# Q and K made in two halves of heads, the second half between the first head's maximum chunks

## What is computed

```
x = x + graph0(norm(x))            # adj @ (norm(x) * W)
h = norm(norm(x)) * g + b
q, k, v = h @ wq + bq, h @ wk + bk, h @ wv + bv     # 8 heads of 32 columns
attn = softmax(q @ k.T / sqrt(32)) # for each head, 1354 x 1354
x = x + ... + (attn @ v) @ wo + bo, then a mixture of 8 experts
x = x + graph1(norm(x)), x = x + experts(norm(x))
```

## Time and profile before

| what | value |
|---|---|
| three runs | 1010.37 us median (1009.64 to 1010.59) |
| the profiled execution's own time | 1012.66 us |
| its span in the trace | 1010.9 us |
| PE, DVE, ACT, POOL busy | 828.1, 518.7, 385.4, 104.5 us |
| granted TensorE clock, mean | 0.899 |

### The profile page before, as it was taken

One profiled execution on the slowest core, in us unless ns is written; L12 is line 12 of the kernel. 1 busy time (PEld: TensorE's weight loads), 2 busy tenths in 40 slices (PEclk: granted clock), 3 DMA queues, 4 the chain that ended last, 5 costly groups with the idle time before them and its releaser, 6 DMA issues.

```text
span 1010.9 us, 12855 instructions
## 1 busy us (share of the span) xinstructions
PE 828.1 (82%) x3873; PEld 578.3 (57%) x3874; DVE 518.7 (51%) x1075; ACT 385.4 (38%) x788; POOL 104.5 (10%) x92
## 2 busy tenths in 40 slices
PE   4968799999999996229999456974449999999993
PEld 4855555555555435129999354862316666666663
DVE  4035587666666748628889237966412222222220
ACT  1004415556555564006666234312013444444441
POOL 2000000000000000160000310000621111111111
PEclk9998859999999999659999777997569999999996
DMA  7498720233321110042442473407231222222212
GB/s 260 148 274 306 209 51 19 69 79 72 77 71 27 36 29 9 10 150 94 166 177 103 144 300 128 143 21 312 78 109 28 32 33 34 32 32 32 32 26 65
DMA packets 53654, 101.57 MB, mean 100 GB/s; under 512 B 17614, under 2 KB 46054, under 8 KB 51920
## 3 DMA queue, kind: packets, MB, share of 16 engines
q1 hardware_dynamic: 47328, 92.20, 28.6%
q0 software_dynamic: 6288, 8.89, 4.9%
HBM read 70.80 MB, written 25.35 MB: 95 GB/s over the span
## 4 chain that ended last, share of the span: by engine, by line
PE 72%; issue 10%; DVE 8%; DMA 4%; ACT 2%; POOL 1%; SPq 0%; POOLq 0%; ACTq 0%; DVEq 0%
PE ps L1167 11%; PE ps L929 11%; PE ps L1149 10%; PE ps L909 6%; PE ps L860 5%; PE ps L921 5%; PE ps L1098 4%; PE ps L1014 4%; PE ps L1016 3%; PE ps L1015 3%; PE ps L1158 3%; DVE mx L1306 2%; PE ps L1113 1%; PE ps L848 1%; PE ps L1075 1%
## 5 line engine op out<-in xcount | busy, mean ns | idle before, releaser
L1306 DVE TENSOR_REDUCE mx<-ps 128x1 f32<-128x452 f32 x264 | 148.1, 621 | 67.3 <-PE ps L909 66.0
L715 ACT ACTIVATE expo<-ps 128x452 f32<-128x452 f32 x264 | 124.3, 551 | 110.4 <-PE ps L921 109.5
L929 PE MATMUL ps<-expo,v_st 128*64 128x452 f32 (+1 forms) x576 | 116.4, 526 | 0.0
L1167 PE MATMUL ps<-w_l,h 128*128 x464 | 110.4, 392 | 7.2 <-ACT h L831 4.1
L909 PE MATMUL ps<-k_st,q_st 96*128 96x452 f32 x264 | 111.3, 451 | 3.5 <-DMA k_st<-k_hi_d 3.3
L831 ACT ACT_TABLE_LOAD x29 | 37.2, 1283 | 190.6 <-PE ps L1158 190.6
L1149 PE MATMUL ps<-w_l,x1t_t 128*128 x232 | 106.0, 600 | 1.7 <-DVE x1t_t L1600 1.7
L1167 PEld LDWEIGHTS ps<-w_l,h 128*128 128x128 f32 x464 | 87.7, 194 | 25.8 <-issue 14.6
L921 PE MATMUL ps<-q_st,k_st 98*128 98x452 f32 x264 | 96.7, 387 | 2.0 <-ACT expo L715 2.0
L1612 DVE COPY h1pre<-ps 128x1024 f32<-128x1024 f32 x29 | 35.5, 1225 | 107.4 <-PE ps L1149 107.4
L909 PEld LDWEIGHTS ps<-k_st,q_st 96*128 96x128 f32 x264 | 54.4, 207 | 50.5 <-DVE mx L1306 35.1
(11 more groups left out here) (230 smaller groups left out, 1233.2 us busy)
## 6 DMA issues: line engine op xcount, KB each, us to landing
w_l<-w_l SPq DMA_DIRECT2D x8, 2053.0 KB, 8.4
w_l<-w_l SPq DMA_DIRECT2D x2, 8208.0 KB, 23.6
adj<-adj_t SPq DMA_DIRECT2D x22, 704.0 KB, 4.2
xs_d<-zeros SPq DMA_DIRECT2D x1, 3842.5 KB, 26.3
x1t<-xs_d SPq DMA_DIRECT2D x29, 132.5 KB, 2.1
q_st<-q_hi_d SPq DMA_DIRECT2D x16, 176.0 KB, 3.2
k_st<-k_hi_d SPq DMA_DIRECT2D x16, 176.0 KB, 4.2
xs_d<-zeros SPq DMA_DIRECT2D x1, 2176.0 KB, 10.5
```

The costliest lines, as they stand in the source:

```text
L715: act.activation(expo[g % 8][:, :], ps[:, 3 + g % 3, 0:QC], ACT.Exp, scale=SCALE).then_inc(s_exp, 1)
L929: return pe.matmul(ps[at:at + 2 * DK, 6 + g // T % 2, lo:hi], v_st[h % 2][:, kt, :], expo[g % 8][:, lo:hi], start=kt < 2, stop=kt == T - 1 ...
L1167: mm = pe.matmul(ps[:, 6, 0:D], h1[:, f, :], w_l1[:, bass.ds(e, 1), at:at + D].rearrange("p a n -> p (a n)"), start=f == 0, stop=f == FT - 1)
L1306: dve.tensor_reduce(mx4[:, n // KB, n % KB:n % KB + 1], ps[:, i % 3, 0:KC], AX_X, ALU.max).then_inc(s_mx, 1)
```

## The change

Q's and K's chunks are ordered by block of heads: eight chunks of heads 0 to 3 (HALF), then eight of heads 4 to 7. All tiles of a chunk have three buffers.

- First half: ACT writes `proj_hi` from PSUM at once, and DVE makes `proj_lo` from PSUM with one scalar_tensor_tensor (bias added, high part subtracted). `proj` isn't written. ACT waits for the stores of the chunk three places earlier.
- SP waits for the first half's stores alone and loads stacks 0 and 1. V's products follow the first half's on PE.
- Second half: PE makes a product, then four maximum slots of head 0 (BESIDE), and so on eight times; then the ten slots that are left. ACT writes `proj` and `proj_hi`, two instructions a chunk, and GpSimd subtracts. These stores stand on SP behind `load_values`, and stack 2 behind them and behind `load_max(0)`.
- ACT loads the table of exponentials ahead of the second half (a 128x1 Exp), waits for all stores ahead of the first exponentials, and PE waits for all high parts ahead of the first scores.

```diff
+        qk_chunks = [(hi_d, lo_d, mt, c) for mt in range(DT) for hi_d, lo_d in ((q_hi_d, q_lo_d), (k_hi_d, k_lo_d))
+                     for c in range(QB)]
+        HALF = len(qk_chunks) // 2
+        def qk_bank(n):
+            return n if n < HALF else 3 + (n - HALF) % 5
+        BESIDE = 4
...
+            for n in range(HALF):
+                store_qk(n)
+            stored(HALF)
...
             load_values(1, 1)
+            for n in range(HALF, 2 * HALF):
+                store_qk(n)
+            load_max(0)
             load_stack(2)
-            load_max(0)
...
-            pool.wait_ge(s_v_ps, T)
+            for n in range(HALF, 2 * HALF):
+                pool.wait_ge(s_qk_hi, n + 1)
+                pool.tensor_tensor(proj_lo[n % 3][:, :], proj[n % 3][:, :], proj_hi[n % 3].bitcast(F32)[:, :],
+                                   ALU.subtract).then_inc(s_qk_lo, 1)
...
+            def qk_high(n):
                 act.wait_ge(s_qk_ps, n + 1)
+                if n >= 3:
+                    act.wait_ge(s_qk_out[n % 3], 32 * (n // 3))
+                for lo, hi, bank in qk_pieces(n):
+                    if n >= HALF:
+                        act.activation(proj[n % 3][:, lo:hi], ps[:, bank, 0:hi - lo], ACT.Identity, bias=qk_bias(n))
+                    last = act.activation(proj_hi[n % 3][:, lo:hi], ps[:, bank, 0:hi - lo], ACT.Identity, bias=qk_bias(n))
+                last.then_inc(s_qk_hi, 1)
...
+            act.activation(psum_e[:, 0:1], ones[:, 0:1], ACT.Exp).then_inc(s_table, 1)
+            for n in range(HALF, 2 * HALF):
+                qk_high(n)
+            act.wait_ge(s_table, 1)
+            for k in range(3):
+                act.wait_ge(s_qk_out[k], 32 * len(range(k, 2 * HALF, 3)))
...
-            for i in range(FILL):
+            for n in range(HALF, 2 * HALF):
+                qk_product(n)
+                for i in range((n - HALF) * BESIDE, (n - HALF + 1) * BESIDE):
+                    fill_slot(i)
+            for i in range(HALF * BESIDE, FILL):
                 fill_slot(i)
+            pe.wait_ge(s_qk_hi, 2 * HALF)
...
+            def qk_low(n):
                 dve.wait_ge(s_qk_hi, n + 1)
+                for lo, hi, bank in qk_pieces(n):
+                    last = dve.scalar_tensor_tensor(out=proj_lo[n % 3][:, lo:hi], in0=ps[:, bank, 0:hi - lo], scalar=qk_bias(n),
+                                                    in1=proj_hi[n % 3].bitcast(F32)[:, lo:hi], op0=ALU.add, op1=ALU.subtract)
+                last.then_inc(s_qk_lo, 1)
```

More of the change, by code:

```diff
@@ L185, in build_program @@
         cursor[0] = offsets["expo0"]
-        proj = [place(f"proj{i}", [NC4]) for i in range(2)]
-        proj_hi = [place(f"proj_hi{i}", [NC4], F32R) for i in range(2)]
-        proj_lo = [place(f"proj_lo{i}", [NC4], F32R) for i in range(2)]
+        proj = [place(f"proj{i}", [NC4]) for i in range(3)]
+        proj_hi = [place(f"proj_hi{i}", [NC4], F32R) for i in range(3)]
+        proj_lo = [place(f"proj_lo{i}", [NC4], F32R) for i in range(3)]
         assert cursor[0] <= offsets["ctx_raw0"]
@@ L290, in build_program @@
         s_qk_ps = sem("qk_product_done")
-        s_qk_raw = sem("qk_biased")
         s_qk_hi = sem("qk_high_ready")
+        s_table = sem("exp_table_wanted")
         s_qk_lo = sem("qk_low_ready")
-        s_qk_out = [sem(f"qk_written{i}") for i in range(2)]
+        s_qk_out = [sem(f"qk_written{i}") for i in range(3)]
         s_v_ps = sem("v_product_done")
@@ L392, in build_program, with qk_pieces, qk_bias @@
         s_b2_add = sem("b2_added")
-        qk_chunks = [(hi_d, lo_d, mt, c) for hi_d, lo_d in ((q_hi_d, q_lo_d), (k_hi_d, k_lo_d))
-                     for mt in range(DT) for c in range(QB)]
+        qk_chunks = [(hi_d, lo_d, mt, c) for mt in range(DT) for hi_d, lo_d in ((q_hi_d, q_lo_d), (k_hi_d, k_lo_d))
[3 more added lines that the diff above has]
+            return n if n < HALF else 3 + (n - HALF) % 5
+        def qk_pieces(n):
+            hi_d, lo_d, mt, c = qk_chunks[n]
+            if hi_d is q_hi_d or c < QB - 1:
+                return ((0, NC4, qk_bank(n)),)
+            return ((0, N - c * NC4, qk_bank(n)), (N - c * NC4, NC4, qk_bank(n - c)))
+        def qk_bias(n):
+            hi_d, lo_d, mt, c = qk_chunks[n]
+            v = (V_BQ if hi_d is q_hi_d else V_BK) + mt
+            return vecs[:, v:v + 1]
         w_l0_b2 = [b[:, FT:FT + DT] for b in b_l0]
@@ L693, in _ @@
             turned(0, V_G1, V_B1)
-            for n, (hi_d, lo_d, mt, c) in enumerate(qk_chunks):
-                v = V_BQ if hi_d is q_hi_d else V_BK
+            def qk_high(n):
                 act.wait_ge(s_qk_ps, n + 1)
[L699 to L704, removed]
-                if pads:
-                    last = act.activation(proj[n % 2][:, real:NC4], ps[:, (n - c) % 8, 0:NC4 - real], ACT.Identity,
-                                          bias=vecs[:, v + mt:v + mt + 1])
-                last.then_inc(s_qk_raw, 1)
+                if n >= 3:
[5 more added lines that the diff above has]
+                last.then_inc(s_qk_hi, 1)
+            for n in range(HALF):
+                qk_high(n)
             def exps(g):
```

38 lines of the change are left out of this document (21 added, 17 removed).

## The result

The changed kernel takes 995.63 us (median of 4 runs, 994.92 to 998.45), the kernel before 1010.0 on the same chip (1007.89 to 1010.59). The ratio is 0.9865, with a 95% interval of 0.9846 to 0.9884: 14.4 us or 1.35% faster. The forecast was 994.5, in 991.5 to 999.5. So its gain by the medians is 14.4 us in the one measurement and 11.4 in the other. The profiled execution took 995.35 us for a span of 993.6, against a span of 1010.9 before. Two executions further on, one of direct16 (1477.88 us) and one of stack2 (2149.08), count in the medians but not in the ratios, and why they were slow is open.

A forecast was written before the change was run, and what follows sets the result against it. Two stretches ahead of the attention, not set by the matmul rate, bound the kernel: stores, then row maxima. Scores 13.4 us earlier plus 2.5 by the clock made 15.9, giving 994.5 us from the median, range 991.5 to 999.5.

The forecast's parts named there:

- first rival: The forecast itself, clock full throughout: 994.5 us, own range 993 to 996; chance 0.50.
- The first stack's issue: First half of Q and K: last store lands at 99.4, so the first stack is issued 15.9 us earlier.
- Issue to first slot: Path from the first stack's issue to PE's first slot: kept at 6.83 us, first slot at 106.2.
- PE's waits: Before the first slot, V and one product keep PE busy until 106.0, so it waits for about nothing.
- Rival 4: PE waits over 3 us for the stack and falls to half clock: 1000.2 to 1008.2 us; chance 0.08.
- Slots with products between: Head 0's slots: seven products between them lose 0.4 us each, 2.8 in all; bounds nothing to 14.
- GpSimd, chunk 15, the table, stack 2: Off the path: subtraction 0.9 us, chunk 15 lands at 128.8 with 3 us cover, table loaded early, stack 2 needed later.
- rival 7: Second half's stores land late and hold up the first exponential, making the kernel slower; chance 0.03.
- The clock at the first scores: First score to second group of value products: at full clock 7.2 us instead of 9.75, gaining 2.5.
- the row of 388 to 391: Sign for a full clock through the last 14 slots: PE busy 1.12 of 3 us there, yet at 1.00.
- rival 2: Clock falls in the last 14 slots, scores begin at half clock: 2.5 us less gain, 997.0; chance 0.24.
- The sum: Whole kernel: 13.4 us from earlier first scores plus 2.5 from the clock, 15.9 us faster.

The follow-up runs named there:

- direct16: Kernel before plus only the three buffers and direct casts, all 16 chunks in the old order: 1004.72 us against 1009.53, ratio 0.9947.
- stack2: Changed kernel with stack 2 loaded ahead of head 0's maxima, as before the change: 998.49 us, ratio 0.9896 to the kernel before.
- again: Changed kernel measured once more, unchanged: 997.28 us against 1008.66 for the kernel before, ratio 0.9892.
- first: Changed kernel with all second-half products ahead of the slots, not between them: 1002.13 us, ratio 0.9928 to the kernel before.
- dvelow: Changed kernel with the second half's low parts made by DVE from PSUM between the maxima: 997.22 us, ratio 0.9886 to the kernel before.
- b3warm: Changed kernel with three slots between products and an added product behind each of the last 18 slots: 990.96 us, ratio 0.9824 to the kernel before.
- notable: Changed kernel without the early Exp that loads the exponential table: 998.02 us, ratio 0.9903 to the kernel before.
- beside5: Changed kernel with five slots between products instead of four: 996.56 us, ratio 0.9881 to the kernel before.
- w0late: b3warm with the first two 2 MB loads of second-layer expert weights moved behind the stacks: 990.11 us, ratio 0.9816 to the kernel before.
- buf2: Changed kernel with two buffers instead of three for the high, low and biased tiles: 1000.53 us, ratio 0.9919 to the kernel before.
- beside3: Changed kernel with three slots between products instead of four: 992.6 us, ratio 0.9851 to the kernel before.
- warm: Changed kernel with one added, unread product behind each of the last ten slots: 993.01 us, ratio 0.9846 to the kernel before.

## Why the prediction was right, and where not

The time was forecast at 994.5 and came at 995.6 and 997.3, in the range and on the side that was said. Two of its steps were off, and the measured times lie between its first rival and its second.

**The first stack's issue.** Forecast 15.9 us earlier; behind Q's first product it is 15.75 earlier (30.56 - 14.81), and 17.2 in again. The step stands, and its parts do: the waits for buffers stayed, with chunk 3 at ACT at 91.02 behind a landing. Nine more executions of the same first half (`first`, dvelow to b3warm, again and notable) show 13.4 to 15.0, so the size is known to 1.5 us and no better. In first and beside5, with 14.98 and 14.90, ACT waited for no landing and a half clock at Q's start set the pace; in the others it was the landing ahead of chunk 3. direct16 and w0late show what makes it up: cheaper casts and buffers 6.2, halves 9.6, and 0.3 (against 13.41 in again) to 1.7 still held by stores.

**Issue to first slot, "I keep it".** A step that was mis-sized: 8.03 instead of 6.83. Where PE waits for the stack at all, it is 8.03 (after), 7.75 (buf2), 7.62 (notable), 7.43 (b3warm), 7.33 (beside3) and 7.10 (direct16). The chain of the kernel after, at the stack:

```profile
98.60 0.32 SPq L504
...
100.35 1.58 SPq L506
101.97 4.62 DMA k_st<-k_hi_d
106.63 0.48 PE ps L946
```

The issues take 3.37 us of SP's time, to 101.97, where they took 2.52 before (115.30 to 117.82), since the one at 100.35 took 1.58 where others take 0.42; the landing takes 4.62 where it took 4.17. That is 1.3 us, of which 0.1 came back at the slot. Why that issue took longer is open.

**PE's waits.** PE waited 1.65 us for the stack in the profile of after, and not at all in again: the forecast, with V and one product ending at 106.0, 21.3 behind Q's first, has the right floor (some 21, as w0late shows), and a stack issued more than about 13.5 behind it is late. Rival 4 stayed out in this kernel. buf2 shows it in one round: 1.54 us, against the 1.6 that rival 4 was priced at. The price was right, and the condition wasn't: the clock fell there behind a wait of 1.39 us, not over 3, while in the changed kernel it stayed at 1.00 through a wait of 1.65. The length of that one wait doesn't decide it, and what does is open; buf2 had a second idle of PE, of 1.62 us ahead of V's later products at 100.51, which the kernel after had not.

**Slots with products between.** Forecast 2.8 us, measured 3.1 (25.18 - 22.07), 0.44 in each of seven rounds of 2.59. The working was right in kind, as beside3 shows: the 0.4 is the price of starting a product one slot after the ring was full. With one slot less it falls to 1.55 us in all.

**GpSimd, chunk 15, the table, stack 2.** The subtraction takes 0.93 us, forecast 0.9. The last low part was issued at 127.35, and ACT's first exponential waited for PE's scores, not for a store (133.16, in the timeline above); rival 7 didn't occur. The table's price is 1.28 us and hidden. stack2 shows that putting the maxima first gives 2.5 us. The forecast counted nothing for it, and rightly: the edit removes a cost that the halves would have brought. The table was loaded early at no cost, as forecast. One sum of rival 7 is off: with rounds of 15 us the last one ends at 108.8 + 45 = 153.8, 21.8 behind 132, and 994.5 + 21.8 is 1016, not 1014. Nothing hangs on it.

**The clock at the first scores: the step that failed.** It was taken at full, for a gain of 2.5 us, on the row of 388 to 391, 1.12 of 3 us busy at 1.00. In all nine profiles with halves and without added products (after, again, first, dvelow, stack2, beside3, beside5, buf2 and notable) it was down when the scores came; it fell 3.2 to 5.5 us after the last product. In the three with added products (warm, b3warm, w0late) it stayed at 1.00. So rival 2 is what happened, with its sum of 13.4 and 997.0. The price was right: warm has 7.33 us from the first score to value 2, forecast 7.2, which is 3.0 less than the changed kernel's 10.31 and 2.2 less than again's 9.54. What went wrong is the reading of that row. Timeline of the kernel before, behind it:

```profile
391.80 3.72 PE L969 MATMUL ps<-w_attn,nt 128*128 128x256 f32 x16 [2.68 <-DVE nt L1334]
```

The row holds the end of one dense run and a single idle of 2.68 us before the next, not single slots for 7.5 us, so it wasn't a row for slots. The Trainium skill, "TensorE: Matmul & The Clock Gate", section "HAM oscillation — how this bites in real kernels", says that idle gaps are what costs the clock. Here it fell in slots that came every 0.54 us, with no idle of PE over 0.79 us in the kernel after and 0.28 in beside3, and one more matmul of 0.2 us in each slot held it.

**The sum.** The first score came 11.7 us earlier instead of 13.4: 0.15 less at the stack, 1.2 by the path to the slot and 0.3 by the slots, the rest as forecast. From there to value 2 it was 0.56 longer instead of 2.5 shorter. That makes the 11.1 of the table. In again the first score came 13.55 us earlier, as forecast, and from there it was 0.2 shorter: 13.8 (69.96 - 56.20), so there the clock's term is the whole miss. The medians say 14.4 and 11.4. Two traces of one kernel differ by 2.6 us up to value 2, and the experts' stage alone moves by 2.8. Taken together the traces give 12.4 and the medians 12.9, so the sum of 15.9 was about 3 us too high, and most of that is the clock's term. That the first measurement came within 1.1 us of the forecast is luck; the second, 997.3, stands at rival 2.

## What to carry to other kernels

When a stage ends in a load that needs all of a product's stores, ask what the first load really needs, and order the work by that: half of the heads were enough here, and the other half's products fit between slots of an engine that waited. Long work for PE goes into a ring at the point where the ring has just been filled, not one slot later: in beside3 that was 1.6 us of 3.1. And look at what comes behind a light stretch: ten slots without company cost the dense stage after them 2.2 to 3.0 us by the clock, and ten small added matmuls gave that back in the trace.

## What the runs showed of the hardware

- TensorE's clock fell from 1.00 to 0.50 between 3.2 and 5.5 us after the last dense product (nine profiles), in slots of one matmul every 0.54 us, where such a matmul takes 0.2 us at full clock (the step from 153.08 to 153.29). It didn't rise in 22.7 us of such slots at half clock. With a second matmul of 0.2 us a slot it stayed at 1.00 (warm, b3warm, w0late).
- It stayed at 1.00 through an idle of 1.65 us in the kernel after, and fell 1.2 us behind the end of one of 1.39 us at the same place in buf2.
- The same program entered the experts' stage at a clock of 0.50 in one execution and 0.89 in another, which moves the whole by 2.8 us. A difference of less than that between two single profiles, in a stage that a change doesn't touch, shows nothing.
- A transfer of 11 KB was there 2.4 us after its issue when it went ahead of six larger ones (beside5, 131.31 to 133.71, where PE waited for it), and 4.3 us after it behind them on the same queue (stack2).
- The load of ACT's table ran ahead of a wait and was hidden in the kernel before, and ran behind the wait and cost 1.28 us in notable.
- GpSimd subtracts 128x352 elements in 0.93 us, and DVE's add-and-subtract from PSUM of the same size takes 0.58.
